# Attention in one-head loops, with 13 of 16 key tiles turned on VectorE and the exchange of their blocks shared out over DMA, GpSimd and ScalarE's queue

## The chip, the cores and the metric

One NeuronCore of a Trainium2 chip runs the whole kernel. The metric is the device time in microseconds (us). The kernel before took 3308.22 us, the median of three runs (3308.05 to 3309.66).

## The reference

`x` is (2, 2048, 256): two batches of 2048 tokens, 4096 tokens in all. The output is `x + attention(layernorm(x)) + moe(layernorm(x))`, all in float32.

    Q, K, V  = xn @ W_{Q,K,V} + b              # 16 heads of 64
    attn     = softmax(Q K^T / 8)              # per head, 2048 x 2048, no mask
    out      = sum over heads (attn V) W_O + b_O
    routed   = for each token, 8 of 32 experts, each row of `ye` times its weight, summed
    shared   = silu(xn Wg) * (xn Wu) Wd

The change concerns attention, and the summing of the 8 expert rows of each token, which GpSimd does beside it.

## The kernel before

The kernel has three stages: `project_and_route` (layer norm, Q, K, V, routing), `run_experts`, and `attend`. Q and K are kept in DRAM as a high and a low part, each float32r; the expert outputs are the rows of `ye`.

`attend` goes through 2 batches x 16 heads x 16 tiles of 128 queries: 512 slots, one per query tile. Each engine has its own program, and they meet at semaphores. `slots` (L846) says what a slot `s` of a head holds; work that lags is of earlier tiles. `over_heads` (L870) writes out the first and the last head of a batch and puts the 14 between into a loop of 7 rounds of two heads.

In one slot:

- TensorE (`body`, L1093): `transpose` turns the last 4 of the 16 key tiles of the probabilities of tile s-2 into bank 7 (L1056); `score` makes the 128 x 2048 scores with 8 matmuls of 512 columns (L1043), the early half into banks 0 and 1 or 4 and 5 by turns, the late half into banks 2 and 3; `project` multiplies the attention output of one tile of 13 slots ago with W_O, also in bank 7 (L1088), as two matmuls of 64 output partitions over 128 rows, which hold the sums over even and over odd key tiles; `times_v` (L1060) multiplies 4 key tiles with V for a group of 4 query tiles (512 queries), even key tiles into partitions 0 to 63 and odd ones into 64 to 127 of bank 6 (L1073).
- VectorE: the maximum over the early and the late half (L1164), the negated maximum (L1169), and the turning of 32 x 32 blocks of the first 12 key tiles of the tile before (`turn_blocks`, L1180). In one slot of four also two small operations on sums (L1195, L1198).
- ScalarE: scaling of the projected tile (L1136), the exponential of the late half (L1124), the copy of the transposed tiles out of bank 7 (`take`, L1112), the exponential of the early half, and in one slot of four the copy of the V product (L1152).
- GpSimd: adds the scaled tile to the accumulator `acc` (L1003), and `routed` (L967): in slots 0 to 7 of a head one indirect DMA each gathers rows of `ye` (L979), in slots 8 to 15 one such tile is multiplied by its weight (L987) and added (L989). Only in slots 8 and 12 does it wait for gathers.
- SyncE's queue: all loads, and `exchange` (L908). A VectorE block transpose stays within its 32 partitions, so block (r, c) of each tile has to go from partitions 32r to partitions 32c. For each group of 4 query tiles that is 16 DMAs of 32 partitions (L914), the 4 with r = c among them. The product with V waits for them one slot after its first part.

`wait_apart` (L37) is a wait followed by a separate semaphore instruction; L44 is its line.

Of the kernel before, what the change touches and what calls it, by code (L numbers as in the profile page):

```python
# [5 lines left out]
F32 = mybir.dt.float32  # L6
# [586 lines left out]
def run_experts(nc, io, scr, keep, ahead, start):  # L593
    with ExitStack() as stack:
# [28 lines left out]
        def _(sp):  # L623
# [9 lines left out]
            for part in range(2):  # L633
                load_k(sp, scr, start, 0, 0, 0, part)
# [126 lines left out]
MOVED = 12  # L761
# [3 lines left out]
LAST = OUT_LAG + TILES  # L765
PV_PLACES = ((12, 16), (0, 4), (4, 8), (8, 12))
# [3 lines left out]
PV_BANK, TURN_BANK = 6, 7  # L770
# [10 lines left out]
def load_k(sp, scr, start, b, h, side, part):  # L781

    keys = slice(part * T // 2, (part + 1) * T // 2)
    sp.dma_start(start["k_hl"][:, side, keys].bitcast(F32),
                 scr["k"][bass.ds(h * P, P), b * T + part * T // 2:b * T + (part + 1) * T // 2]
                 ).then_inc(start["k_loaded"][side], 16)


def attend(nc, io, scr, keep, ahead, start):
    with ExitStack() as stack:  # L790
# [8 lines left out]
        oT = ahead["xe"][:, 0, :, :].rearrange("p t d -> p (t d)").rearrange("p (g c) -> p g c", c=CH)  # L799
# [15 lines left out]
        scaled_sb = m.sb("scaled", [P, 2, D])  # L815
# [10 lines left out]
        exchanged = m.sems("exchanged", 2)  # L826
        turned = m.sem("turned")
# [18 lines left out]
        def slots(b, h):  # L846


            i, u = h if isinstance(h, tuple) else (0, h)
            h = 2 * i + u  # L850
            head = b * H + h
            pair, side = b * (H // 2) + i + u // 2, u % 2
            opens = b == 0 and isinstance(h, int) and h == 0
            for s in range(LAST if b == B - 1 and isinstance(h, int) and h == H - 1 else TILES):
# [4 lines left out]
                out = not opens or s >= OUT_LAG  # L859
                yield dict(  # L860
                    s=s, h=h, head=head, tile=tile, scores=s < TILES, side=side, pair=pair,
                    out_side=1 - side if s < OUT_LAG else side, out_pair=pair - 1 if s < OUT_LAG and not side else pair,
                    turn=(head * GROUPS + back[0], back[0] % 2, (s - 1) % GT) if turn and s <= TILES else None,
                    late=(not opens or s >= 2) and s <= TILES + 1,
                    pv=(head * GROUPS + back[1], back[1] % GROUPS, (s - PV_LAG) % GT)
                    if pv and s < PV_LAG + TILES else None,
                    out=(head * GROUPS + back[2], back[2] % GROUPS, (s - OUT_LAG) % GT, s < OUT_LAG)
                    if out and s < OUT_LAG + TILES else None)

        def over_heads(eng, body):  # L870
            for b in range(B):
                for s in slots(b, 0):
                    body(b, 0, s)
                with eng.Fori(0, H // 2 - 1) as i:
                    for u in (1, 2):
                        for s in slots(b, (i, u)):
                            body(b, (i, u), s)
                for s in slots(b, H - 1):
                    body(b, H - 1, s)

        def exchanges(head, g):

            return (head * (GROUPS // 2) + g // 2 + 1) * (QD * QD * 16)

        @block.sync
        def _(sp):
# [5 lines left out]
            def next_k(b, h, side, part):  # L892
                wait_apart(sp, late_scored, (b * H + h - 1) * TILES, sp_waits)
                load_k(sp, scr, start, b, h, side, part)
# [8 lines left out]
            def load_wo(b, h, side):  # L903
                wait_apart(sp, projected, (b * H + h - 1) * TILES + 1, sp_waits)
# [3 lines left out]
            def exchange(b, h, g):  # L908
# [9 lines left out]
            def store_out(b):  # L918

                for t in range(TILES):  # L920
                    sp.wait_ge(added, ((b + 1) * H - 1) * TILES + t + 1)
# [3 lines left out]
            def head_loads(b, h, side, before, following):  # L925

                next_q(b, h, 1)
                if before is not None:
                    exchange(*before, GROUPS - 1)
# [3 lines left out]
                load_wo(b, h, side)  # L933
# [3 lines left out]
                if following is not None:  # L937
                    next_k(*following, 1 - side, 0)
                exchange(b, h, 1)
                if following is not None:  # L940
                    next_q(*following, 0)
                    next_k(*following, 1 - side, 1)
                exchange(b, h, 2)

            for b in range(B):
                head_loads(b, 0, 0, (b - 1, H - 1) if b else None, (b, 1))
                with sp.Fori(0, H // 2 - 1) as i:
                    for u in (1, 2):
                        head_loads(b, 2 * i + u, u % 2, (b, 2 * i + u - 1), (b, 2 * i + u + 1))
                head_loads(b, H - 1, 1, (b, H - 2), (b + 1, 0) if b + 1 < B else None)  # L950
# [5 lines left out]
        def _(pool):  # L956
# [10 lines left out]
            def routed(b, s):  # L967

                k, h, n = s["s"] % K, s["h"], s["head"]
                part = k // (K // 2)  # L970
                if s["s"] < K:
                    if k == 0:
                        tile = b * TILES + h
                        nc.gpsimd.tensor_copy(g_index[:, :], keep["index"][:, bass.ds(tile, 1), :]
                                              .rearrange("p a k -> p (a k)"))
                        nc.gpsimd.tensor_copy(g_gain[:, :], keep["gain"][:, bass.ds(tile, 1), :]
                                              .rearrange("p a k -> p (a k)")).then_inc(g_staged, 1)
                        wait_apart(pool, g_staged, n + 1, pool_waits)
                    nc.gpsimd.indirect_dma_start(  # L979
# [303 lines left out]
```

## Time and profile before

| | us |
|---|---|
| median of 3 runs | 3308.22 |
| the profiled execution itself | 3313.78 |
| its span, first to last instruction | 3312.2 |
| TensorE busy (97% of the span) | 3196.9 |
| VectorE busy (77%) | 2544.1 |
| ScalarE busy (61%) | 2007.7 |
| GpSimd busy (44%) | 1454.5 |

Busy time is what an engine's own operations cover; waits, branches and the issue of DMAs on SyncE are not in it. The profiled execution took 5.6 us more than the median of the runs, 1.6 us of its time lie around the span.

### The profile page before, as it was taken

To read this page: it belongs to the slowest core of one execution; us is meant where nothing else is said; L and a number is where in the kernel's file an instruction comes from. 1 tells how busy PE (TensorE), PEld (TensorE's weight loads), DVE (VectorE), ACT (ScalarE), POOL (GpSimd) and SP (SyncE) were. 2 spreads that over 40 slices of the span, in tenths; PEclk is the share of its full clock that TensorE was granted. 3 is DMA by queue.
4 is the path that set the end of the run, shared out by engine and by line. 5 is a ranking of instruction groups with operands and counts; after the bars stand their busy time and mean duration, and the time that the engine had idled before them with its cause. 6 is when DMAs were issued, how large, how long until landed. Compare 5 with 4: busy or idle time off the path is not lost.

```text
span 3312.2 us, 54697 instructions
## 1 busy us (share of the span) xinstructions
PE 3196.9 (97%) x14467; PEld 1714.4 (52%) x14468; DVE 2544.1 (77%) x2917; ACT 2007.7 (61%) x3525; POOL 1454.5 (44%) x1795
## 2 busy tenths in 40 slices
PE   7799999998999999999999999999999999999998
PEld 3355444555555555555555555555555555555554
DVE  7612444234998989898988999898999899889995
ACT  4312320334676767676766777777777777777775
POOL 4677770013244444444444445544444444444443
PEclk9899999999999999999999999999999999999999
DMA  7613886665998989898988899999999999899997
GB/s 299 266 68 117 309 267 153 223 228 187 236 236 216 231 214 229 212 231 219 229 218 218 216 233 243 261 231 226 231 230 230 229 230 228 219 225 232 227 227 183
DMA packets 342733, 737.33 MB, mean 223 GB/s; under 512 B 129517, under 2 KB 177400, under 8 KB 342160
## 3 DMA queue, kind: packets, MB, share of 16 engines
q1 hardware_dynamic: 311056, 670.55, 76.9%
q0 software_dynamic: 31488, 64.51, 7.0%
q8 instruction: 88, 1.44, 0.2%
q14 instruction: 101, 0.83, 0.1%
HBM read 198.37 MB, written 159.51 MB: 108 GB/s over the span
## 4 chain that ended last, share of the span: by engine, by line
PE 70%; DVE 2%; issue 1%; SPq 1%; ACT 1%; DMA 0%; ACTq 0%; POOL 0%; DVEq 0%; POOLq 0%
PE at_ps L1043 27%; PE at_ps L1073 26%; PE at_ps L1056 9%; PE at_ps L1088 9%; DVE at_half_max L1164 1%; DVE at_blocks L1180 1%; SPq L914 1%; ACT at_prob L1124 0%; DMA at_v<-v_rows 0%; DMA at_moved<-at_blocks 0%; ACT at_scaled L1136 0%; DVE at_neg_max L1169 0%; ACT ahead_xe L1152 0%; SPq L905 0%; POOL at_acc L1003 0%
## 5 line engine op out<-in xcount | busy, mean ns | idle before, releaser
L1164 DVE TENSOR_REDUCE at_half_max<-at_ps 128x1 f32<-128x1024 f32 x1024 | 1206.6, 1219 | 250.9 <-PE at_ps L1043 249.0
L1124 ACT ACTIVATE at_prob<-at_ps,at_neg_max 128x1024 f32<-128x1024 f32 x1024 | 1145.3, 1118 | 333.7 <-DVE at_neg_max L1169 318.3
L1180 DVE STREAM_TRANSPOSE at_blocks<-at_prob 128x1536 f32<-128x1536 f32 x512 | 906.0, 1770 | 1.2 <-ACT at_prob L1124 1.2
L1043 PE MATMUL at_ps<-ahead_k_hl,ahead_q_hh 128*128 128x512 f32 x2048 | 854.4, 417 | 17.7 <-ACT at_prob L1124 10.8
L1003 POOL TENSOR_TENSOR at_acc<-at_acc,at_scaled 128x256 f32<-128x256 f32 x512 | 372.0, 727 | 1064.0 <-ACT at_scaled L1136 1064.0
L1043 PE MATMUL at_ps<-ahead_k_hl,ahead_q_ll 128*128 128x512 f32 x2048 | 810.2, 396 | 0.0
L1073 PE MATMUL at_ps<-at_moved,at_v 128*64 128x512 f32 x3072 | 726.8, 594 | 5.6 <-DMA at_moved<-at_blocks 4.3
L1136 ACT ACTIVATE at_scaled<-at_ps,at_inv 128x256 f32<-128x256 f32 x512 | 242.3, 473 | 354.1 <-PE at_ps L1088 340.0
L1056 PEld LDWEIGHTS at_ps<-keep_ident,at_prob 128*128 128x128 f32 x2048 | 216.1, 141 | 437.9 <-issue 425.5
L1043 PEld LDWEIGHTS at_ps<-ahead_k_hl,ahead_q_hh 128*128 128x128 f32 x2048 | 389.4, 190 | 88.2 <-ACT at_prob L1124 15.5
L1043 PEld LDWEIGHTS at_ps<-ahead_k_hl,ahead_q_ll 128*128 128x128 f32 x2048 | 390.4, 191 | 67.7
L1073 PEld LDWEIGHTS at_ps<-at_moved,at_v 128*64 128x64 f32 x3072 | 221.1, 137 | 282.4 <-issue 221.1
L1056 PE MATMUL at_ps<-keep_ident,at_prob 128*128 128x128 f32 x2048 | 337.0, 287 | 26.5 <-issue 21.1
L1088 PE MATMUL at_ps<-ahead_dn,ahead_xe 128*64 128x256 f32 x2048 | 336.1, 407 | 4.0 <-ACT at_scaled L1136 2.4
L1112 ACT COPY at_turned_sb<-at_ps 128x512 f32<-128x512 f32 x512 | 300.5, 587 | 44.4 <-PE at_ps L1056 35.2
L286 POOL DMA_INDIRECT xbuf<-pr_ebase,pr_stage_i x256 | 249.6, 975 | 100.3 <-issue 72.3
L1073 PE MATMUL at_ps<-at_turned_sb,at_v 128*64 128x512 f32 x1024 | 248.3, 604 | 2.5 <-issue 2.0
L1088 PEld LDWEIGHTS at_ps<-ahead_dn,ahead_xe 128*64 128x64 f32 x2048 | 102.9, 135 | 192.1 <-issue 187.9
L1124 ACT ACTIVATION_READ_ACCUMULATOR at_prob<-at_ps,at_neg_max 128x1 f32 x1024 | 201.6, 197 | 0.0
L979 POOL DMA_INDIRECT ahead_gu<-ye,at_g_index x128 | 133.8, 1045 | 115.0 <-POOL at_acc L1003 75.8
L979 POOL DMA_INDIRECT ahead_xe<-ye,at_g_index x128 | 131.6, 1028 | 108.8 <-POOL at_acc L1003 103.3
L645 POOL DMA_DIRECT2D ye<-ex_ye x32 | 24.2, 756 | 274.4 <-ACT ex_ye L664 271.2
(112 smaller groups left out, 2596.1 us busy)
## 6 DMA issues: line engine op xcount, KB each, us to landing
at_moved<-at_blocks SPq DMA_DIRECT2D x2048, 192.0 KB
ahead_k_hl<-k_parts SPq DMA_DIRECT2D x64, 512.0 KB, 8.0
ahead_q_hh<-q_parts SPq DMA_DIRECT2D x128, 256.0 KB, 5.6
ahead_q_ll<-q_parts SPq DMA_DIRECT2D x128, 256.0 KB, 6.4
xbuf<-pr_zeros SPq DMA_DIRECT2D x32, 512.0 KB, 5.1
q_parts<-pr_part_hi SPq DMA_DIRECT2D x64, 256.0 KB
q_parts<-pr_part_lo SPq DMA_DIRECT2D x64, 256.0 KB
k_parts<-pr_part_hi SPq DMA_DIRECT2D x64, 256.0 KB, 2.2
```

The costliest lines, as they stand in the source:

```text
L286: nc.gpsimd.indirect_dma_start(out=scr["xbuf"][:, :], out_offset=bass.IndirectOffsetOnAxis(ap=stage_i[:, q, k:k + 1], axis=0), in_=stage_x ...
L979: nc.gpsimd.indirect_dma_start(out=row(k), out_offset=None, in_=scr["ye"][:, :], in_offset=bass.IndirectOffsetOnAxis(ap=g_index[:, k:k + 1 ...
L1003: nc.gpsimd.tensor_tensor(acc[:, t, :], acc[:, t, :], scaled_sb[:, t % 2, :], ALU.add).then_inc(added, 1)
L1043: last = nc.tensor.matmul(ps[:, bank, :], q[:, g % 2, j * P:(j + 1) * P], k_hl[:, side, c * CH:(c + 1) * CH], start=first, stop=not first)
L1056: last = nc.tensor.transpose(ps[:, TURN_BANK, j * P:(j + 1) * P], prob[:, s["s"] % 2, t * P:(t + 1) * P], keep["ident"][:, :])
L1073: last = nc.tensor.matmul(ps[side:side + DH, PV_BANK, :], v[:, t, :], p_T, start=(place == 0 and t < tiles[0] + 2), stop=(place == GT - 1 ...
L1088: last = nc.tensor.matmul(ps[side:side + DH, TURN_BANK, 0:D], oT[:, g % 2, j * P + side:j * P + side + DH], wo[:, s["out_side"], :], start ...
L1112: nc.scalar.copy(turned_sb[:, parity, :, :, j, :], ps[:, TURN_BANK, 0:TURNED * P].rearrange("p (t r c) -> p t r c", r=QD, c=32)).then_inc( ...
L1124: nc.scalar.activation(prob[:, i % 2, half * 1024:(half + 1) * 1024], ps[:, banks[0]:banks[1], :].rearrange("p b c -> p (b c)"), ACT.Exp, ...
L1136: nc.scalar.activation(scaled_sb[:, t % 2, :], ps[:, TURN_BANK, 0:D], ACT.Identity, scale=inv[:, t:t + 1]).then_inc(scaled, 1)
L1164: nc.vector.tensor_reduce(half_max[:, i % 2, half:half + 1], ps[:, banks[0]:banks[1], :], AX.XY, ALU.max).then_inc(max_step, 1)
L1180: nc.vector.transpose(blocks[:, parity, :, j, :, :].rearrange("p c t k -> p t c k"), prob[:, (s["s"] - 1) % 2, 0:MOVED * P].rearrange("p ( ...
```

## The change

- The loop over the heads has one head per round, 14 rounds a batch. So both buffers of K (and of W_O) are loaded for each head: side 0 serves tiles 0 to 7, side 1 tiles 8 to 15.
- VectorE turns 13 of 16 key tiles, TensorE 3. TensorE turns them for two query tiles at once, in even slots, into banks 4 and 5, and ScalarE copies both in one instruction. Bank 7 is no longer used.
- The V product puts the first half of a group's queries into partitions 0 to 63 and the second half into 64 to 127: 256 columns per matmul and twice as many matmuls. The four slots take 3, 5, 4 and 4 key tiles.
- The projection of a query tile is one matmul over 64 rows with 128 output partitions. Two of them (rows 0 to 63 and rows 64 to 127) are made in each odd slot, into the two banks of the early half that is free.
- GpSimd copies the 4 diagonal blocks of a group, two in each even slot. It issues its gathers in pairs in even slots, and waits for each pair at the start of the next even slot.
- Of the 12 DMAs that are left, SyncE's queue issues the 6 with r = 0, 1 and ScalarE's queue the 6 with r = 2, 3, two at the end of each of three slots.

```diff
-MOVED = 12
+MOVED = 13
-PV_PLACES = ((12, 16), (0, 4), (4, 8), (8, 12))
+PV_PLACES = ((13, 16), (0, 5), (5, 9), (9, 13))
+GQ = GT // 2
+UPPER = ((2, 0), (3, 1), (2, 1), (3, 0), (2, 3), (3, 2))
-def load_k(sp, scr, start, b, h, side, part):
+def load_k(sp, scr, start, b, h, side):
...
-                with eng.Fori(0, H // 2 - 1) as i:
-                    for u in (1, 2):
-                        for s in slots(b, (i, u)):
-                            body(b, (i, u), s)
+                with eng.Fori(1, H - 1) as h:
+                    for s in slots(b, h):
+                        body(b, h, s)
...
-                for turn in range(QD):
+                for turn in range(1, QD):
                     for r, c in zip(ACROSS, ACROSS[turn:] + ACROSS[:turn]):
+                        if r >= QD // 2:
+                            continue
                         sp.dma_start(moved[c * 32:(c + 1) * 32, g % 2, r, :, :, :],
...
+            def diagonal(group, parity, r):
+
+                wait_apart(pool, blocks_done, GT * (group + 1), pool_waits)
+                wait_apart(pool, pv_done, GT * (group - 1), pool_waits)
+                for q in (r, r + 1):
+                    nc.gpsimd.tensor_copy(moved[q * 32:(q + 1) * 32, parity, q, :, :, :],
+                                          blocks[q * 32:(q + 1) * 32, parity, q, :, :, :]).then_inc(diag_done, 1)
+                    wait_apart(pool, diag_done, QD * group + q + 1, pool_waits)
...
+                if i % 2 == 0 and 0 < i <= K:
+                    part = (i - 1) // (K // 2)
+                    wait_apart(pool, gathered[part], s["head"] * 64 + 16 * (i - part * (K // 2)), pool_waits)
+                if s["diag"]:
+                    diagonal(*s["diag"])
...
+                    pe.wait_ge(diag_done, QD * (group + 1))
                     pe.wait_ge(exchanged[parity], exchanges(s["head"] - (1 if s["s"] < PV_LAG else 0), g))
...
+                    for half in range(2):
+                        side, queries = half * DH, slice(half * GQ, (half + 1) * GQ)
+                        p_T = (moved[:, parity, :, queries, t, :] if t < MOVED else
+                               turned_sb[:, parity, t - MOVED, :, queries, :])
+                        last = nc.tensor.matmul(ps[side:side + DH, PV_BANK, 0:GQ * P], v[:, t, :], p_T,
...
+                for n, g, j, half, behind in s["out"]:
...
+                    rows, queries = slice(half * DH, (half + 1) * DH), slice(j % GQ * P, (j % GQ + 1) * P)
+                    nc.tensor.matmul(out_of(s, half), oT[rows, g % 2, queries], wo[rows, g // 2, :],
+                                     start=True, stop=True).then_inc(projected, 1)
...
+            def send_upper(group, parity, part):
+
+                act.wait_ge(blocks_done, GT * (group + 1))
+                wait_pos(act, pv_done, GT * (group - 1))
+                for r, c in UPPER[2 * part:2 * part + 2]:
+                    nc.scalar.dma_start(moved[c * 32:(c + 1) * 32, parity, r, :, :, :],
+                                        blocks[r * 32:(r + 1) * 32, parity, c, :, :, :]).then_inc(exchanged[parity], 16)
```

GpSimd's order in an even slot is: the wait for the pair of gathers (slots 2, 4, 6, 8), two diagonal copies, then a pair of gathers (slots 0 to 6) or two times multiply and add (slots 8 to 14). In an odd slot it adds two scaled tiles. In the kernel before, the accumulator of scaled tiles `scaled_sb` has 2 buffers, in the changed one 4.

## Rows read from the trace of the kernel before

**Rows 1.** The page: busy time of each engine, then shares of the last chain.
```profile
PE 3196.9 (97%) x14467; PEld 1714.4 (52%) x14468; DVE 2544.1 (77%) x2917; ACT 2007.7 (61%) x3525; POOL 1454.5 (44%) x1795
...
PE 70%; DVE 2%; issue 1%; SPq 1%; ACT 1%; DMA 0%; ACTq 0%; POOL 0%; DVEq 0%; POOLq 0%
```
**Rows 2.** Windows: length, busy time of each engine, clock, DMA share over attention's slots.
```profile
805.00:3272.00 2467.00, 2427.01 (x12145) 1318.25 (x12143) 2202.88 (x2295) 1760.40 (x3177) 1086.43 (x1372) 0.99 0.92 227
```
**Rows 3.** Timeline of TensorE over a slot: start, length, instruction.
```profile
2273.06 0.66 PE L1056 MATMUL at_ps<-keep_ident,at_prob 128*128 128x128 f32 x4
...
2277.79 0.66 PE L1056 MATMUL at_ps<-keep_ident,at_prob 128*128 128x128 f32 x4
2278.20 0.47 PE L1043 MATMUL at_ps<-ahead_k_hl,ahead_q_hh 128*128 128x512 f32 x1
...
2279.90 0.39 PE L1043 MATMUL at_ps<-ahead_k_hl,ahead_q_ll 128*128 128x512 f32 x1
2280.22 0.65 PE L1088 MATMUL at_ps<-ahead_dn,ahead_xe 128*64 128x256 f32 x4
2280.71 1.94 PE L1073 MATMUL at_ps<-at_turned_sb,at_v 128*64 128x512 f32 x8
```
**Rows 4.** Timeline of VectorE in the first head, before V products begin.
```profile
833.29 2.31 DVE L1164 TENSOR_REDUCE at_half_max<-at_ps 128x1 f32<-128x1024 f32 x2
...
835.77 1.77 DVE L1180 STREAM_TRANSPOSE at_blocks<-at_prob 128x1536 f32<-128x1536 f32 x1
837.46 1.19 DVE L1164 TENSOR_REDUCE at_half_max<-at_ps 128x1 f32<-128x1024 f32 x1
```
**Rows 5.** Timeline: TensorE's first work after a loop's jump, batch 0, then batch 1.
```profile
1186.30 1.04 PE L1056 MATMUL at_ps<-keep_ident,at_prob 128*128 128x128 f32 x4 [3.64 <-issue]
...
2284.24 0.66 PE L1056 MATMUL at_ps<-keep_ident,at_prob 128*128 128x128 f32 x4 [1.60 <-ACT at_scaled L1136]
```
**Rows 6.** GpSimd's groups by form: its copies of 256 and of 8 elements.
```profile
L282 POOL COPY pr_ebase<-pr_xn 128x256 f32 x30 | 12.4, 412 | 0.0
...
L280 POOL COPY pr_stage_i<-keep_index 128x8 uint32 x30 | 6.4, 214 | 0.0
```
**Rows 7.** Timeline of GpSimd: a routed slot, a gather, two scatters in a row.
```profile
2340.43 0.73 POOL L1003 TENSOR_TENSOR at_acc<-at_acc,at_scaled 128x256 f32<-128x256 f32 x1 [1.94 <-ACT at_scaled L1136]
2341.46 0.93 POOL L987 TENSOR_SCALAR ahead_xe<-ahead_xe,at_g_gain 128x256 f32<-128x256 f32 x1 [0.30 <-POOL at_acc L1003]
2342.59 0.73 POOL L989 TENSOR_TENSOR at_acc<-at_acc,ahead_xe 128x256 f32 x1 [0.20 <-POOL ahead_xe L987]
...
2366.01 1.02 POOL L979 DMA_INDIRECT ahead_gu<-ye,at_g_index  x1 [0.88 <-POOL at_acc L1003]
...
389.39 0.97 POOL L286 DMA_INDIRECT xbuf<-pr_ebase,pr_stage_i  x1 [0.30 <-issue]
390.66 0.97 POOL L286 DMA_INDIRECT xbuf<-pr_ebase,pr_stage_i  x1 [0.30 <-issue]
```
**Rows 8.** DMA issues of one later head, then of the first: KB, us to landing.
```profile
DMA packets 5468, 17.16 MB, mean 226 GB/s; under 512 B 1376, under 2 KB 2016, under 8 KB 5467
...
at_moved<-at_blocks SPq DMA_DIRECT2D x64, 192.0 KB
...
ahead_k_hl<-k_parts SPq DMA_DIRECT2D x2, 512.0 KB, 7.6
...
ahead_xe<-ye,at_g_index POOLq DMA_INDIRECT x4, 6.4
...
ahead_xe<-ye,at_g_index POOLq DMA_INDIRECT x4, 3.3
```
**Rows 9.** Timeline of SyncE's queue: issues of the exchange in a row.
```profile
2283.89 8.09 SPq L914 DMA_DIRECT2D at_moved<-at_blocks  x12
```
**Rows 10.** The page's groups of ScalarE: scaling and copy of the transposed tiles.
```profile
L1136 ACT ACTIVATE at_scaled<-at_ps,at_inv 128x256 f32<-128x256 f32 x512 | 242.3, 473 | 354.1 <-PE at_ps L1088 340.0
...
L1112 ACT COPY at_turned_sb<-at_ps 128x512 f32<-128x512 f32 x512 | 300.5, 587 | 44.4 <-PE at_ps L1056 35.2
```

More of the change, by code:

```diff
@@ L630, in load @@
                     load_expert(sp, io, scr, ahead, e, q)
-            for part in range(2):
-                load_k(sp, scr, start, 0, 0, 0, part)
+            load_k(sp, scr, start, 0, 0, 0)
             load_q(sp, scr, start, 0, 0, 0)
@@ L995, in body @@
+                if i == 0 and not first and not last:
                     for q in range(4):
                         pool.wait_ge(base_loaded[q], 64 * (b + 1))
-                if s["out"]:
-                    group, g, j, behind = s["out"]
-                    n, t = group * GT + j, g * GT + j
-                    if h == 0 and not behind:
+                if b == 1 and first and i % GT == 1:
+                    g = i // GT
+                    for t in range(g * GT, (g + 1) * GT):
+                        pool.wait_ge(first_stored[t % 4], 16 * (t // 4 + 1))
+                        load_base(1, t)
@@ L1005, in body @@
                     wait_apart(pool, added, n + 1, pool_waits)
[L1006 removed]
+                    if b == 0 and last and not behind or b == 1 and first and behind:
                         store_first(t)
[L1008 to L1014 removed]
@@ L1076, in times_v @@
                 last.then_inc(pv_done, 1)
             def project(s):
-                group, g, j, behind = s["out"]
-                n = group * GT + j
-                if j == 0:
-                    pe.wait_ge(oT_done, group + 1)
-                    pe.wait_ge(wo_loaded[s["out_side"]], 16 * s["out_pair"] + 16)
-                wait_pos(pe, scaled, n)
-                if s["late"]:
-                    pe.wait_ge(copied, s["tile"] - 1)
-                for side in (0, DH):
-                    last = nc.tensor.matmul(ps[side:side + DH, TURN_BANK, 0:D],
-                                            oT[:, g % 2, j * P + side:j * P + side + DH], wo[:, s["out_side"], :],
-                                            start=True, stop=True)
@@ L1091, in project @@
-                last.then_inc(projected, 1)
+                for n, g, j, half, behind in s["out"]:
+                    if j == 0:
+                        pe.wait_ge(oT_done, s["pv_group"])
+                        pe.wait_ge(wo_loaded[g // 2], 16 * (s["head"] + (0 if behind else 1)))
+                    if half == 0:
+                        pe.wait_ge(early_exp, min(s["s"], TILES) + s["head"] * TILES)
+                        wait_pos(pe, scaled, n)
+                    rows, queries = slice(half * DH, (half + 1) * DH), slice(j % GQ * P, (j % GQ + 1) * P)
+                    nc.tensor.matmul(out_of(s, half), oT[rows, g % 2, queries], wo[rows, g // 2, :],
+                                     start=True, stop=True).then_inc(projected, 1)
@@ L1098, in body @@
                     score(s, 1)
-                if s["out"]:
-                    project(s)
+                project(s)
+                if s["taken"]:
+                    transpose(s)
                 if s["pv"]:
```

211 lines of the change are left out of this document (106 added, 105 removed).

## The prediction

> **What bounds the kernel now.** I read the page first: TensorE is busy for 97% of the span, and 70% of the chain that ended last is TensorE's own work [rows 1]. The windows then say the same of attention alone: 2427 of 2467 us, against 2203 for VectorE, 1760 for ScalarE, 1086 for GpSimd, with the DMA engines 92% busy [rows 2]. That window holds 511 slots, 4.83 us each. The timeline of a slot shows where TensorE's time lies: one slot begins at 2273.06 and the next at 2277.79, 4.73 us; in it the transposes take 0.41, the scores 2.02, the projection 0.49, and the V product the other 1.81 [rows 3]. The 0.10 us between 4.73 and 4.83 are mostly pauses at the loops' jumps. In batch 0 TensorE stood still for 3.64 us with nothing to wait for but its own instructions, and its first transposes then took 1.04 us in place of 0.66, as at 1.2 GHz; in batch 1 it waited 1.60 us on ScalarE [rows 5]. There are 6 such jumps in each batch. GpSimd, 44% busy, seems far from any limit. That is the reading I have to test, because it is the engine that the change loads most.
>
> **TensorE, four slots.** Scores 4 x 2.02 = 8.08, unchanged. Transposes: 12 instead of 16, at 0.41/4 = 0.10 each: 1.24. Projection: today 4 x 0.49, two matmuls of 256 columns side by side each time. The new pairs are side by side in rows and no longer in columns; the trace has no such pair. If they overlap likewise, two pairs cost 0.98, if they follow each other 2 x 0.9. I take 0.98, since they go to different rows and different banks as today's go to different columns. V product: the same columns in all, 4 x 1.81 = 7.24; the matmuls become half as long, and 256-column pairs already follow each other at 0.49 for two of them [rows 3], so the shorter form costs nothing that rows show. From the last score (2279.90) to the projection are 0.32 us, against 0.24 between scores: a change of shape costs 0.08. Odd slots get one more, 0.16 in four. Sum 8.08 + 1.24 + 0.98 + 7.24 + 0.16 = 17.7, or 4.43 per slot (4.65 if the pairs don't overlap).
>
> **VectorE.** In the first head, where it had no idle time, its slot was 833.29 to 837.46, 4.17 us [rows 4]. The transposes grow from 1536 to 1664 elements: 1.77/12 = 0.15 more. Two small operations in one slot of four add under 0.1 on average. So 4.4, beside TensorE's 4.43. As the two alternate and each waits for the other at times, I take 4.5 for both together.
>
> **ScalarE.** The copies of the transposed tiles become one of 768 elements for two slots, about 0.85 where two took 1.17, and the scalings stay [rows 10]. It issues 24 DMAs a head; SyncE's queue needs 8.09/12 = 0.67 us for each [rows 9]. Two follow the early exponential, in three slots of four. An issue keeps the sequencer busy and not the arithmetic, and the exponential that it follows lasts over a microsecond, so I cost it at nothing; uncovered it would be at most 6 x 0.67 = 4.0 us in four slots, of which the pause before the next maximum takes up about 1 us a slot. Still about 4.5 to 4.7. SyncE's queue gets shorter.
>
> **DMA.** A head moves 17.16 MB [rows 8]. 64 exchanges of 192 KB become 48 of 208 KB, 12.58 to 10.22 MB; the second load of K adds 1.05 and that of W_O 0.13: 16.0 MB. At 92% busy before, that is about 0.86 at the old pace and under 0.8 at 82 us a head. It bounds nothing. Each part of the exchange has more than a slot until it is read.
>
> **GpSimd.** Here the sum must be made in wall time, since each of its operations waits for the one before. Row by row:
> - Odd slot: two adds of 0.73 with 0.30 between them (two waits) and 0.15 ahead: 1.9 [rows 7].
> - Diagonal copies: 32 partitions, but 1664 elements in each. 256 elements took 0.412 and 8 took 0.214 [rows 6], that is 0.80 ns an element, so 0.412 + 1408 x 0.80 = 1.54. Short copies overlap a little, so the true slope is higher. I take 1.6. The ends: 1.4, were all of the 0.214 overlap, and 6.0, were it as slow per element as the multiply (0.93 for 256 [rows 7]); the copy's own row is the nearest. Two copies, 0.2 between, and 0.45 for the waits ahead of them (0.30 is seen for two): 3.85 per even slot.
> - Even slot 8 to 14: two multiplies and adds, 2 x (0.2 + 0.93 + 0.2 + 0.73) = 4.1.
> - Even slot 0 to 6: 0.88 until the first gather, 1.28 until the second (the scatters' spacing), 1.02 for it [rows 7]: 3.2.
>
> So two slots cost 3.85 + 4.1 + 1.9 = 9.85 in the second half of a head and 3.85 + 3.2 + 1.9 = 8.95 in the first, with 0.4 for the index copies: 75.6 us for 16 slots. TensorE needs 16 x 4.5 = 72. GpSimd is then the bound, although its busy share would look like 75%. The diagonal copies of a group must be done before the second of the four V products; a lag that grows each half head soon reaches that wait.
>
> To this comes a new wait. Before, gathers were waited for only half a head later, so their landing cost nothing. Now the pair issued in slots 0, 2, 4, 6 is waited for at the start of the next even slot, ahead of the copies. The second gather starts 3.85 + 0.88 + 1.28 = 6.0 us into its pair of slots; the next pair begins when it has landed, at 6.1 + L. Landing took 6.4 us in a later head and 3.3 in the first, when the DMA engines were less loaded [rows 8]. The new load lies between, and the second gather queues behind the first: I take L = 4.5, with 3.3 and 6.4 as ends. Four pairs cost 4 x 10.6 = 42.4. Queued behind this wait are the copies, the adds and with them the V product.
>
> **Sum.** A head costs GpSimd 42.4 + 4 x 9.85 + 0.4 = 82.2 us, 5.14 a slot; 511 slots 2625, less 8 for the first head, where most of this is missing: 2617 against 2467 [rows 2], +150. The pauses at the jumps are in the 2467 and need no term of their own; with TensorE waiting for GpSimd they gain nothing. The stages before attention stay. 3313.8 + 150 = 3464 for the profiled execution, whose time was 5.6 us over the median of the runs; so 3458.
>
> **Rivals.**
> - Landing is quick (L under 3). Then no gather is waited for, a head costs 75.6, and 511 slots 2414 - 8: -61, **3247**. For it: fewer and more evenly spread exchanges. Against it: even the first head had 3.3. The Trainium skill, "DMA: Bandwidth & Descriptors", section "Anatomy of one DMA", gives a DMA of GpSimd's queue about 2.0 us plus its bytes over 436 GB/s, an estimate of 2.3 us for 128 KB, and thus this rival's time. The rows of this trace stand above that figure throughout.
> - TensorE and VectorE remain the bound at 4.5: 511 x 4.5 = 2300, -167, **3141**. That needs a copy on GpSimd of at most (1.6 - 10.2/16) = 1.0 us at L = 4.5. For it: with only 32 of 128 partitions a copy may be cheaper than its elements say. Against it: the rows know only 128 partitions, and elements per partition should count. With row pairs that do not overlap this becomes 4.7, about 3240.
> - Landing as slow as in the later heads (L = 6.4) with copies of 1.7: 4 x 12.7 + 4 x 10.05 + 0.4 = 91.4 a head, +440, **3750**. Three queues instead of two compete with the gathers.
> - The point between faster and slower is a GpSimd head of about 77.5 us (2467/511 x 16 and the first head's 8 us spread): L = 3.3 with copies of 1.6, or L = 4.5 with copies of 1.3.
>
> **How the numbers follow.** The forecast with GpSimd and its gathers as the bound has 0.52, its own range 3330 to 3600 (L 3.5 to 5.5, copies 1.5 to 1.7). Quick landing 0.14, TensorE as the bound 0.22 (with the unpaired projection), slower landing 0.08, a balance near zero 0.04. A measurement of this kernel tells about 0.2% from no change. Faster 0.36, same 0.04, slower 0.60. Both signs hold much, so the range that leaves out 2 in 10 reaches from TensorE's case to 3600.
>
> **What would show it.** Right: copies on GpSimd of 1.5 to 1.7 us; GpSimd's idle time put down to the landing of gathers, in slots 2 to 8; V products waiting for GpSimd's copies, once per group; TensorE's slots at 4.4 between those waits; the even halves of a head (slots 0 to 7) slower than slots 8 to 15; TensorE at 85 to 90% busy. Wrong: copies under 1.1 us, or GpSimd waiting for the scaled tiles as it does now, or V products waiting for the exchange's DMAs or ScalarE.

## The result and the profile after

The changed kernel takes 3685.36 us (median of 4 runs, 3668.17 to 3694.97), the kernel before beside it 3308.14 us: ratio 1.1135, 95% interval 1.1093 to 1.1176. The direction was forecast, the size was not: 3685 lies above the range, which ended at 3600. The profiled execution has a span of 3683.6 us.

The page of the changed kernel, busy times and the chain that ended last:

```profile
PE 3237.7 (88%) x17028; PEld 1972.3 (54%) x17028; DVE 2652.1 (72%) x2917; ACT 1867.8 (51%) x3269; POOL 2259.2 (61%) x2307
...
POOL 27%; DMA 21%; PE 17%; issue 10%; POOLq 2%; ACT 0%; DVE 0%; ACTq 0%; DVEq 0%
POOL at_moved L1009 16%; DMA ahead_xe<-ye,at_g_index 10%; PE at_ps L1103 9%; DMA ahead_gu<-ye,at_g_index 8%; PE at_ps L1071 7%; DMA at_moved<-at_blocks 3%; POOL at_acc L1034 3%; POOL at_acc L1001 3%; POOL ahead_gu L998 2%; POOL ahead_xe L99
```

TensorE had 70% of this chain before [rows 1], now GpSimd and the DMAs that it waits for lead. Attention's slots as one window (same columns as [rows 2]):

```profile
805.00:3640.00 2835.00, 2465.10 (x14615) 1568.30 (x14615) 2302.26 (x2287) 1615.58 (x2912) 1873.81 (x1871) 0.93 0.74 183
```

The window grew from 2467 to 2835 us, +368 of the +377 in all. The DMA engines fell from 92% to 74%, and the mean granted clock from 0.99 to 0.93. A slot took 5.57 us on average, 89.1 us a head (from the starts of VectorE's late maxima, 511 intervals; all slot times below are made so). Over the heads, slots 1, 5 and 9 took 9.27, 7.02 and 11.59 us, and most of the others 4.54 to 4.7: the time was lost in a few long stops. What GpSimd and TensorE waited for (engine, line and cause; us in total, times, longest):

```profile
POOL at_moved L1009 <- DMA ahead_xe<-ye,at_g_index: 230.8, 58, 8.6
POOL at_moved L1009 <- DMA ahead_gu<-ye,at_g_index: 202.6, 59, 5.2
```
```profile
PE at_ps L1103 <- POOL at_moved L1009: 243.0, 68, 11.9
PE at_ps L1103 <- DMA at_moved<-at_blocks: 93.4, 28, 4.4
```

GpSimd stood 433 us before its diagonal copies until gathers had landed, 13.5 us a head. TensorE's V products stood 243 us for those copies, about twice a head. They stood another 93 us for DMAs of the exchange, 28 times and always in slot 1, a sign that the prediction had listed under "wrong". GpSimd's timeline over one head's gathers shows the loop of the stall:

```profile
2310.25 1.57 POOL L1009 COPY at_moved<-at_blocks 32x1664 f32<-32x1664 f32 x1 [0.54 <-POOL at_acc L1034]
2311.99 1.57 POOL L1009 COPY at_moved<-at_blocks 32x1664 f32<-32x1664 f32 x1 [0.17 <-POOL at_moved L1009]
...
2315.20 1.16 POOL L993 DMA_INDIRECT ahead_gu<-ye,at_g_index  x1 [0.91 <-POOL at_g_gain L987]
2316.66 1.03 POOL L993 DMA_INDIRECT ahead_gu<-ye,at_g_index  x1 [0.30 <-issue]
2317.71 0.75 POOL L1034 TENSOR_TENSOR at_acc<-at_acc,at_scaled 128x256 f32<-128x256 f32 x1
2318.79 0.73 POOL L1034 TENSOR_TENSOR at_acc<-at_acc,at_scaled 128x256 f32<-128x256 f32 x1 [0.34 <-POOL at_acc L1034]
2323.70 1.56 POOL L1009 COPY at_moved<-at_blocks 32x1664 f32<-32x1664 f32 x1 [4.18 <-DMA ahead_gu<-ye,at_g_index]
...
2334.88 1.57 POOL L1009 COPY at_moved<-at_blocks 32x1664 f32<-32x1664 f32 x1 [2.76 <-DMA ahead_gu<-ye,at_g_index]
...
2346.82 1.56 POOL L1009 COPY at_moved<-at_blocks 32x1664 f32<-32x1664 f32 x1 [3.50 <-DMA ahead_xe<-ye,at_g_index]
```

Each pair of slots is paced by the landing: 13.45, 11.18 and 11.94 us from copy to copy, and 13.52 for the fourth. The DMA view of the whole run gives the landing (count, median us):

```profile
ahead_gu<-ye,at_g_index POOLq DMA_INDIRECT x128, 5.8
ahead_xe<-ye,at_g_index POOLq DMA_INDIRECT x128, 5.7
```

These medians are over both gathers of a pair, but GpSimd waits for the second one. From issue to landing the second took 6.2 us in the mean of all 128 pairs, and GpSimd's copies began 0.4 us after it had landed.

### The profile page after: what moved, and what is told of

The parts are those of the page before. It is cut to its first block, busy times and chain, and to the rows that moved or that the text cites. A ratio compares the mean times of both kernels' runs of the same rounds, so it can differ in the third digit from the quotient of the medians.

```text
span 3683.6 us, 61395 instructions
## 1 busy us (share of the span) xinstructions
PE 3237.7 (88%) x17028; PEld 1972.3 (54%) x17028; DVE 2652.1 (72%) x2917; ACT 1867.8 (51%) x3269; POOL 2259.2 (61%) x2307
## 4 chain that ended last, share of the span: by engine, by line
POOL 27%; DMA 21%; PE 17%; issue 10%; POOLq 2%; ACT 0%; DVE 0%; ACTq 0%; DVEq 0%
POOL at_moved L1009 16%; DMA ahead_xe<-ye,at_g_index 10%; PE at_ps L1103 9%; DMA ahead_gu<-ye,at_g_index 8%; PE at_ps L1071 7%; DMA at_moved<-at_blocks 3%; POOL at_acc L1034 3%; POOL at_acc L1001 3%; POOL ahead_gu L998 2%; POOL ahead_xe L998 2%; PE at_ps L1083 1%; PE at_ps L1118 1%; POOLq L44 1%; POOL ahead_xe L993 1%; POOLq L43 1%
## 5 line engine op out<-in xcount | busy, mean ns | idle before, releaser
L1103 PE MATMUL at_ps<-at_moved,at_v 128*64 128x256 f32 x6656 | 912.7, 424 | 349.6 <-POOL at_moved L1009 243.0
L1009 POOL COPY at_moved<-at_blocks 32x1664 f32<-32x1664 f32 x512 | 802.1, 1567 | 557.4 <-DMA ahead_xe<-ye,at_g_index 230.8
L1218 DVE STREAM_TRANSPOSE at_blocks<-at_prob 128x1664 f32<-128x1664 f32 x512 | 974.3, 1903 | 200.9 <-POOL at_moved L1009 148.9
L1071 PE MATMUL at_ps<-ahead_k_hl,ahead_q_hh 128*128 128x512 f32 x2048 | 882.7, 431 | 19.2 <-ACT at_prob L1152 8.7
L1103 PEld LDWEIGHTS at_ps<-at_moved,at_v 128*64 128x64 f32 x6656 | 497.1, 150 | 689.5 <-issue 308.9
L1139 ACT COPY at_turned_sb<-at_ps 128x768 f32<-128x768 f32 x256 | 204.8, 800 | 740.5 <-PE at_ps L1083 740.5
L1083 PE MATMUL at_ps<-keep_ident,at_prob 128*128 128x128 f32 x1536 | 211.3, 274 | 1.8 <-ACT at_prob L1152 1.8
L1083 PEld LDWEIGHTS at_ps<-keep_ident,at_prob 128*128 128x128 f32 x1536 | 182.5, 141 | 41.0 <-issue 9.8
L1103 PE MATMUL at_ps<-at_turned_sb,at_v 128*64 128x256 f32 x1536 | 194.8, 389 | 0.5 <-issue 0.5
L1118 PE MATMUL at_ps<-ahead_dn,ahead_xe 64*128 64x256 f32 x1024 | 179.9, 424 | 14.8 <-ACT at_scaled L1164 1.0
```

What stands on the lines that cost most here:

```text
L1009: nc.gpsimd.tensor_copy(moved[q * 32:(q + 1) * 32, parity, q, :, :, :], blocks[q * 32:(q + 1) * 32, parity, q, :, :, :]).then_inc(diag_don ...
L1071: last = nc.tensor.matmul(ps[:, bank, :], q[:, g % 2, j * P:(j + 1) * P], k_hl[:, side, c * CH:(c + 1) * CH], start=first, stop=not first)
L1083: last = nc.tensor.transpose(ps[:, EARLY[1][0] + a, j * P:(j + 1) * P], prob[:, a, t * P:(t + 1) * P], keep["ident"][:, :])
L1103: last = nc.tensor.matmul(ps[side:side + DH, PV_BANK, 0:GQ * P], v[:, t, :], p_T, start=(place == 0 and t == tiles[0]), stop=(place == GT ...
L1118: nc.tensor.matmul(out_of(s, half), oT[rows, g % 2, queries], wo[rows, g // 2, :], start=True, stop=True).then_inc(projected, 1)
L1218: nc.vector.transpose(blocks[:, parity, :, j, :, :].rearrange("p c t k -> p t c k"), prob[:, (s["s"] - 1) % 2, 0:MOVED * P].rearrange("p ( ...
```

## The experiments

The runs were made on several chips. On two of them (the first seven experiments) the kernel before itself took 3445 and 3492 us; there attention only began at 935 to 987 us instead of 800, so the extra time lies ahead of the part studied. The mean slot of attention is therefore the better number to compare across runs, the ratio within one. Three comparisons below still cross chips: e1 with e10, e6 with e8, and e5 with e9. Those of the changed kernel with e13, of e9 with e14 and of e11 with e12 were made where the kernel before took 3308 to 3311 us. The mean slot of e2 is that of its longest execution (3581 us; the other three took 3525 to 3576).

| run | chip's kernel before, us | ratio, 95% interval | mean slot, us |
|---|---|---|---|
| changed kernel | 3308 | 1.1135 [1.1093, 1.1176] | 5.57 |
| e1_gathers_apart | 3445 | 1.0639 [1.0616, 1.0663] | 5.25 |
| e2_diag_dma | 3445 | 1.0318 [1.0244, 1.0392] | 5.10 |
| e3_both | 3445 | 1.0265 [1.0227, 1.0304] | 5.04 |
| e4_two_heads | 3492 | 1.0518 [1.0480, 1.0555] | 5.16 |
| e5_twelve | 3492 | 1.0203 [1.0158, 1.0248] | 4.96 |
| e6_no_gathers | 3492 | 1.0220 [1.0203, 1.0237] | 4.99 |
| e7_half_copies | 3492 | 1.0214 [1.0186, 1.0243] | 4.98 |
| e8_sooner | 3311 | 0.9783 [0.9767, 0.9799] | 4.69 |
| e9_queue | 3311 | 1.0043 [1.0027, 1.0060] | 4.87 |
| e10_apart | 3311 | 1.0295 [1.0277, 1.0312] | 5.03 |
| e11_both_ways | 3311 | 1.0078 [1.0062, 1.0095] | 4.88 |
| e12_one_head | 3308 | 0.9807 [0.9793, 0.9820] | 4.69 |
| e13_sooner_alone | 3308 | 1.0793 [1.0764, 1.0822] | 5.36 |
| e14_twelve_one_head | 3308 | 0.9792 [0.9779, 0.9805] | 4.70 |

### Taking the landing, and the copies, away

**e1_gathers_apart**: the four copies of a group together in slots 0, 4, 8, 12, the gathers four at a time behind them in slots 0 and 4, waited for four slots later.

```diff
-                if i % 2 == 0 and 0 < i <= K:
-                    part = (i - 1) // (K // 2)
-                    wait_apart(pool, gathered[part], s["head"] * 64 + 16 * (i - part * (K // 2)), pool_waits)
+                if i % GT == 0 and 0 < i <= K:
+                    wait_apart(pool, gathered[i // GT - 1], s["head"] * 64 + 64, pool_waits)
```

> The changed kernel with the landing of the gathers taken off GpSimd's path and nothing else: the four diagonal copies of a group stand together in every fourth slot, the gathers go out four at a time right behind them (slots 0 and 4) and are waited for four slots later. Theory A (the changed kernel is bound by GpSimd's own work, 75.6 us a head, plus the landing waits, some 13.5 us a head): the landing waits vanish, a head falls from 89 to about 75 to 77 us, the whole to 3240 to 3300 us, and TensorE still waits for the copies once per group. Theory B (the landing waits only stand where something else, such as the exchange's DMAs or the half clock of TensorE, is the bound): the time stays above 3550.

**e2_diag_dma** sends the diagonal blocks by SyncE's DMAs as before and keeps the waits for pairs of gathers; **e3_both** also moves these waits to slots 8 and 12.

```diff
-                for turn in range(1, QD):
+                for turn in range(QD):
...
-                        if r >= QD // 2:
+                        if turn and r >= QD // 2:
```

> The changed kernel with the 4 diagonal blocks sent by SyncE's queue like the others, no copies on GpSimd; the waits for the pairs of gathers stay. Theory A: GpSimd has about 8.5 us of work and landing in two slots of the first half head and 6.4 in the second, both under TensorE's 9, so TensorE and VectorE bound it at 4.5 us a slot: 3130 to 3180 us. Theory B (DMA or the new waits on TensorE bind): over 3400, with V products waiting for the exchange, which now has a third more blocks.

> Diagonal blocks by DMA as in e2 and the gathers waited for only where they are used (slots 8 and 12), as in the kernel before. Theory A: the same as e2 within 0.5%, as neither wait is on the path any more: 3130 to 3180 us, faster than the kernel before by about 5%. If landing still held up the adds of the scaled tiles in e2, e3 is faster than e2 by more than 0.5%.

In e1 the waits for landing went, and the slot fell from 5.57 to 5.25, but not to GpSimd's own 75.6 us a head (4.73): it came to 84, with slots 1 and 5 at 8.42 and 6.69. In e2 and e3 GpSimd makes no copies, and in e3 no landing is waited for until the rows are used either, yet slot 1 still took 9.47 and 9.16, and V products waited 148 us in e3 for DMAs of the exchange. TensorE at 4.5 was not reached, and something in slot 1 was left that is neither copies nor landing. As e3's DMA engines showed 99% busy at 245 GB/s, I took the bytes for it:

```profile
1000.00:3500.00 2500.00, 2343.64 (x14360) 1502.19 (x14358) 2192.39 (x2225) 1575.30 (x2845) 1054.79 (x1332) 0.97 0.99 245
```

### Bytes, or something else?

**e4_two_heads** is e3 with two heads a round, so K and W_O are loaded once a head; **e5_twelve** is e4 with

```diff
-MOVED = 13
+MOVED = 12
...
-PV_PLACES = ((13, 16), (0, 5), (5, 9), (9, 13))
+PV_PLACES = ((12, 16), (0, 4), (4, 8), (8, 12))
```

> The kernel of e3_both (13 tiles, diagonals by DMA, gathers waited for late) with the loop over two heads again, so K and W_O are loaded once a head: 19.34 - 1.05 - 0.13 = 18.16 MB a head. Theory that the bytes bind once GpSimd is relieved: at the 245 GB/s that e3_both reached a head takes 74 to 76 us, a slot 4.65 to 4.75 us, DMA engines still 98 to 99% busy, ratio to the kernel before about 0.98. Rival, that the load of K just ahead of the exchange delays it by its place in the queue: slots of 4.55, DMA share under 0.96, ratio 0.96. Rival, that the DMA issues on ScalarE or TensorE itself set 5.0: no change from e3_both, ratio 1.03.

> e4_two_heads with 12 tiles turned on VectorE and 4 on TensorE, as in the kernel before: 17.16 MB a head, as before. Theory of the bytes: 17.16 MB at 245 GB/s are 70 us, so TensorE becomes the bound, with one more transpose of 0.10 a slot: 4.6 to 4.7 a slot, ratio 0.965 to 0.975, DMA share 0.95 to 0.97, and faster than e4_two_heads or equal. Rival, that fewer tiles on TensorE pay whatever the DMA does: e4_two_heads is faster than this one by 0.1 us a slot (1.5%).

Both forecasts of the theory of the bytes were missed, 4.65 to 4.75 for e4 and 4.6 to 4.7 for e5. Though 1.2 MB a head lighter, e4 was even slower than e3 (5.16 against 5.04). That alone does not refute the bytes, since the longer loop also brings back the pause at its jump: slot 15 took 6.01 in e4 and 4.55 in e3. What speaks against them is that the stop had moved: slot 13 took 8.44 and slot 1 4.87 in e4. In e5 slots 13 and 15 took 6.51 and 6.31; it was faster than e4, so the rival expected of it fell as well. e14 below settles the point.

**e6_no_gathers** and **e7_half_copies** change only GpSimd's part of the changed kernel. After the first head e6 leaves out the gathers and the waits for them, so the rows added are not those of the tokens; e7 leaves out half of each diagonal copy, so half of these blocks keep old values.

```diff
+                    if s["s"] < K and not opening:
+                        continue
...
+                if b == 0 and first and i % 2 == 0 and 0 < i <= K:
```
```diff
-                    nc.gpsimd.tensor_copy(moved[q * 32:(q + 1) * 32, parity, q, :, :, :],
+                    nc.gpsimd.tensor_copy(moved[q * 32:(q + 1) * 32, parity, q, 0:tiles, :, :],
```

> The changed kernel without its gathers after the first head, and without the waits for them (left out: the routed rows that are added are not those of the tokens). Theory that the landing of the gathers is the error of the forecast: GpSimd's two slots cost 3.85 + 1.9 + 0.3 = 6.05 in the first half of a head and 9.85 in the second, 64 us a head, so TensorE sets the time at 4.55 to 4.7 a slot, ratio to the kernel before 0.95 to 0.975. Rival, that landing only covers something else (ScalarE's DMA issues, the exchange): slots stay above 5.0, ratio above 1.03.

> The changed kernel with half of each diagonal block copied after the first head of a batch (left out: the diagonal blocks of two of a group's four query tiles keep old values). Theory, GpSimd in wall time: each copy loses 832 elements x 0.80 ns = 0.67 us, 16 a head, 89.1 - 10.7 = 78.4 us a head, 4.9 a slot, ratio about 1.02, and the waits for landing stay 12 to 14 us a head. Rival, that a 32-partition copy has a price that doesn't go by its elements: copies stay near 1.5 us and the time near that of the changed kernel, 1.10. Rival, that the landing waits grow as the copies shrink: ratio above 1.06.

Both lost the stops in slots 5 and 9, and both ended at the same place, 4.99 and 4.98: slot 1 took 9.43 and 9.68, all others 4.54 to 5.24. So the stops in slots 5 and 9 go when either the landing or half of the copying is taken away, and slot 1 has another cause. e7's ratio is the one expected, but not for the reason given: its landing waits were 215 us, 6.7 a head instead of 12 to 14, and TensorE's slot 1 made up the rest. The halved copies took 0.87 us each, where the whole one took 1567 ns: 0.84 ns an element. The mean of 886 ns in this line also holds the first head's whole copies:

```profile
L1009 POOL COPY at_moved<-at_blocks 32x832 f32<-32x832 f32 (+1 forms) x512 | 453.4, 886 | 359.1 <-DMA ahead_gu<-ye,at_g_index 113.5 <-DMA ahead_xe<-ye,at_g_index 101.7 <-DVE at_blocks L1218 50.6
```

The timeline of e7 around slot 1 of a head names the cause:

```profile
2083.21 1.83 ACTq L1172 DMA_DIRECT2D at_moved<-at_blocks  x2
...
2089.64 1.16 ACTq L1172 DMA_DIRECT2D at_moved<-at_blocks  x2
...
2094.47 0.34 SPq L784 DMA_DIRECT2D ahead_k_hl<-k_parts  x1
...
2095.55 0.61 ACTq L1172 DMA_DIRECT2D at_moved<-at_blocks  x1
...
2104.95 4.54 PE L1103 MATMUL at_ps<-at_moved,at_v 128*64 128x256 f32 x20 [2.88 <-DMA at_moved<-at_blocks]
```

SyncE's six blocks of the group had left by 2085. ScalarE's six leave by twos in three slots; the last leaves at 2095.55, 1.1 us behind the load of 1 MB of K, and lands 9.4 us later, 2.88 us after TensorE wants it. Then TensorE's product takes 4.54 us, where the same 20 matmuls took 2.38 at 2083.39 of the same head: 634 ns a matmul instead of 379. The granted clock of 2105 to 2109 was 0.50, so 1.2 instead of 2.4 GHz. A wait of 2.9 us thus cost 5.

That the load of K counts, and not the late place alone, shows within e6, e7 and the changed kernel. ScalarE's last two DMAs leave at the same place in slots 3, 7, 11 and 15, but a load of K goes out just ahead of them only in slot 15, and TensorE waited for the exchange in slot 1 alone, 28 times for 90 to 93 us in each of the three. In e4 and e5, with two heads a round, the load just ahead stands in slot 11, and most of these waits lie in slot 13: 82 us in e4 (44 in slot 5 and 32 in slot 9), 42 us in e5.

### Sending sooner

In **e8_sooner** (on e6), **e10_apart** (on e1) and **e13_sooner_alone** (on the changed kernel itself) ScalarE sends three DMAs in each of two slots:

```diff
-                    if (not opens or s >= 5) and s < TILES + 5 and (s - 5) % GT < 3 else None,
+                    if (not opens or s >= 5) and s < TILES + 5 and (s - 5) % GT < 2 else None,
...
-                for r, c in UPPER[2 * part:2 * part + 2]:
+                for r, c in UPPER[3 * part:3 * part + 3]:
```

> e6_no_gathers (the changed kernel without its gathers, the same part left out), and ScalarE's queue sends its six DMAs of a group three each in two slots instead of two each in three. In e6_no_gathers and e7_half_copies nearly all time over 4.7 a slot lies in slot 1, 9.4 to 9.7 us, where TensorE waits about 3 us for an exchange and then runs at half clock: the last two DMAs of group 2 leave ScalarE's queue in slot 15, right behind the second load of K (1 MB), and land 9 us later. Theory that the third of ScalarE's sendings comes too late for its reader: slot 1 falls to 4.6 to 5.5, the mean slot from 4.99 to 4.70 to 4.75, ratio to the kernel before about 0.98. Rival, that the load of K holds up whatever is in flight then: slot 1 stays above 8. Rival, that three issues in a row delay ScalarE's next exponential: all slots of two in four grow by 0.5 or more.

> e1_gathers_apart (all gathers, waited for four slots later, all four copies on GpSimd), and ScalarE's sendings in two slots instead of three. Theory of two separate costs: slot 1 loses its wait of the exchange as in e8_sooner, 3 to 4 us a head, so 5.25 becomes 5.0 to 5.05; what is left over 4.75 (GpSimd's own sum of 75.6 us a head) is GpSimd waiting where four copies and four gathers in a row make it late. Ratio 1.02 to 1.03. Rival, that GpSimd alone sets e1's time: no change, 1.06.

> The changed kernel, and only ScalarE's sendings three each in two slots. Its price over the kernel before was 11.3%. Theory that the late third sending costs it something of its own beside the landing of the gathers (e1_gathers_apart to e10_apart gained 3.4 points, on different chips): 1.08 to 1.10, and slot 1 falls from 9.3 us by 2 to 4. Rival, that GpSimd's head of 89 us sets the time whatever the exchange does, so that ScalarE's delay lies beside it: 1.105 to 1.115, slot 1's time only moves to slots 5 and 9.

In e8 slot 1 fell from 9.43 to 5.27 and the mean to 4.69: the theory held, with its number, though e8 and e6 ran on different chips. In e13, the one change in the changed kernel itself and on a chip like the first, slot 1 fell from 9.27 to 5.97 and the ratio from 1.1135 to 1.0793, just under the range expected; slot 5 rose from 7.02 to 9.48, since part of GpSimd's lateness comes out there. What is left is GpSimd's sum:

```profile
POOL at_moved L1009 <- DMA ahead_xe<-ye,at_g_index: 196.4, 61, 7.5
POOL at_moved L1009 <- DMA ahead_gu<-ye,at_g_index: 132.4, 54, 4.8
```

329 us in 32 heads are 10.3 a head; with 75.6 that is 85.9, measured 85.8. In the changed kernel it is 13.5 + 75.6 = 89.1, measured 89.1. So the landing waits themselves shrank by 3.2 us a head when ScalarE sent sooner, and that is the whole gain of e13. The gathers landed sooner: the second of a pair took 5.4 us in the mean instead of 6.2, and four pairs times 0.8 are 3.2. This was not for a lighter load, since in e13 the DMA engines were 77% busy at 190 GB/s, in the changed kernel 74% at 183. That the late sendings and the gathers are then less often in the DMA engines together is my reading; no run separates it. e10 takes these waits out too: 1.0295, 80.5 us a head, where four copies in a row make V products wait 170 us for GpSimd.

### One queue, and the jump of the loop

**e9_queue** is e5 with all 16 DMAs of a group on SyncE's queue. **e11_both_ways** is e10 with two heads a round, and with two of the four diagonal blocks copied by GpSimd and two sent by DMA. **e12_one_head** is e11, and **e14_twelve_one_head** is e9, each with one head a round again.

```diff
+                        if (r >= QD // 2) == (turn > 0):
+                            continue
...
-                for q in range(QD):
+                for q in range(QD // 2):
```

> e5_twelve (12 tiles, two heads a round, all 16 blocks by DMA, 17.16 MB a head) with all of the exchange on SyncE's queue as in the kernel before; against that kernel only the query halves, the projection by row pairs and the transposes by two are left. Theory that ScalarE's late sendings cost e5_twelve its waits in slots 13 and 15: they go, slots 4.55 and 4.81 by turns, mean 4.70 to 4.75, ratio 0.97 to 0.985. Rival, that the DMA engines are the bound: 17.16 MB at the pace of this chip take as long as in the kernel before, ratio 0.995 to 1.005 and waits for at_moved spread over the slots.

> A version meant to beat both: 13 tiles, two heads a round, gathers in fours waited for four slots later, two diagonal blocks of a group copied by GpSimd and two by DMA, ScalarE's sendings in two slots. GpSimd's sum is 75.6 - 8 x 1.9 = 60 us a head, the bytes 16.0 - 1.18 + 8 x 0.21 = 16.5 MB. If the costs add up as the theory says, neither binds, slots of 4.6 to 4.7, ratio 0.955 to 0.975. Rival, that the DMA engines bind near 17 MB whoever issues: 0.99 to 1.01.

> e11_both_ways with one head a round as in the changed kernel: 16.5 + 1.18 = 17.7 MB a head. In e11_both_ways every second head loses 5 to 6 us in its slot 15, with half clock behind it, where TensorE waits for nothing but its instructions at the loop's jump. Theory that this pause goes with the shorter loop: mean slot 4.88 - 0.17 = 4.71 or a little less, ratio 0.975 to 0.985, faster than both kernels. Rival, that the larger bytes (DMA share above 0.95) bring waits for the exchange back: slots 1 and 13 over 6 us, ratio 0.99 to 1.02.

> e9_queue (12 tiles, all 16 blocks by DMA on SyncE's queue, gathers waited for late) with one head a round: 17.16 + 1.18 = 18.3 MB a head. Theory of the jump: slot 15 falls from 6.87 to 4.6, mean slot 4.70 to 4.75, ratio 0.975 to 0.985. Rival of the bytes: 18.3 MB at 240 GB/s take 76 us a head, 4.77 a slot, so the gain is lost to the DMA engines, ratio 0.985 to 1.00.

From e5 to e9 slot 13 went from 6.51 to 4.70, which fits ScalarE's late sendings as the cause there too (the chip changed as well). Yet e9 is 0.4% slower than the kernel before, as the rival of the bytes had it; but not for the bytes. The same holds for e11, meant to beat both kernels at 0.955 to 0.975 and measured at 1.0078. Its heads take 75.5 and 80.8 us by turns, and the difference lies in slot 15 of every second one, at the loop's jump:

```profile
2430.68 1.95 PE L1104 MATMUL at_ps<-at_moved,at_v 128*64 128x256 f32 x16
2437.13 0.79 PE L1073 MATMUL at_ps<-ahead_k_hl,ahead_q_hh 128*128 128x512 f32 x1 [4.50 <-issue]
2437.72 0.63 PE L1073 MATMUL at_ps<-ahead_k_hl,ahead_q_ll 128*128 128x512 f32 x1
...
2440.27 0.63 PE L1073 MATMUL at_ps<-ahead_k_hl,ahead_q_ll 128*128 128x512 f32 x1
```

TensorE stands 4.50 us with nothing to wait for, 12 times in the run, and then works at half clock (granted 0.50 from 2437 to 2442; 0.63 a matmul, else 0.39). That slot 15 took 10.56 us instead of 4.55. The page counts the DMAs that fetch TensorE's instructions, queue 8 (packets, MB, share), first in e9, then in e14:

```profile
q8 instruction: 159, 2.61, 0.4%
```
```profile
q8 instruction: 31, 0.51, 0.1%
```

With one head a round the fetching and the pause are gone: slot 15 takes 4.56, the mean falls from 4.87 to 4.70, the ratio from 1.0043 to 0.9792 (e11 to e12: 1.0078 to 0.9807). The kernel before has such pauses too, shorter ones [rows 5]: 88 packets, slot 15 at 5.66 us in the mean, where e9 has 6.87. The query halves double the number of V matmuls in the body, which is the likely reason for the longer ones, though no run takes the halves alone. And e14 moves 18.3 MB a head and waits for the exchange 9.2 us in all:

```profile
805.00:3199.00 2394.00, 2377.26 (x15166) 1575.02 (x15166) 2198.83 (x2292) 1647.83 (x2918) 1083.09 (x1368) 1.00 0.97 248
```
```profile
PE at_ps L1097 <- DMA at_moved<-at_blocks: 9.2, 4, 4.6
```

97% busy and 248 GB/s, and TensorE still has 2377 of 2394 us. So the DMA share of 99% in e3 did not by itself prove a bound; what counts is when a block leaves.

Both e12 and e14 came out as their theories had it and are faster than both kernels, by 2% over the kernel before (3242.36 and 3238.38 against 3307.79). They keep the change's one-head loop, query halves, row-pair projection and transposes by two. e14 needs neither GpSimd's copies nor ScalarE's queue.

## Why the prediction was wrong

**Right.** The reading of GpSimd as the new bound in wall time, at 61% busy. Its copies took 1.57 us (I took 1.6), a routed pair of slots 10.0 (9.85), and the head without landing 75.6, in the changed kernel as in e13. V products waited for GpSimd's copies, about twice a head where I had four times. On GpSimd the first half of a head was the slower one, as I had it, 49.3 against 40.4 us; by TensorE's slots the halves came out alike, 44.6 and 44.5 us, since the lag that the gathers leave comes out in slot 9. TensorE's row pairs overlap: the four matmuls of an odd slot take 0.63 us until the V product starts (e9's and e14's timelines; I had 0.49, and 0.9 if they followed each other).

**The step that failed** is "I take L = 4.5, with 3.3 and 6.4 as ends". The four pairs of the head shown took 50.1 us, where I had 42.4: (50.1 / 4) - 6.1 gives L = 6.4, my upper end, and the second gathers of these pairs took 5.3 to 7.7 us to land, 6.4 in the mean. Over all heads they took 6.2, so the sum lacks 4 x (6.2 - 4.5) = 6.8 us a head. What is missing is 89.1 - 82.2 = 6.9 us a head, 32 heads 221 us: nearly the whole of 3685 - 3458 = 227. I had argued that a lighter DMA load brings the landing between the two rows of before [rows 8]. The load did become lighter (74% instead of 92%), but the landing hardly shorter: a median of 5.7 us for the gathers into `ahead_xe`, 6.6 before. And the busy share does not order it: in e14, at 97%, the medians were 5.6 and 5.7, in e13, at 77%, about 4.8. Why a gather takes what it takes stays open beyond what e13 shows. The Trainium skill, "DMA: Bandwidth & Descriptors", section "Anatomy of one DMA", would give 2.3 us for these 128 KB, an estimate; the trace does not agree, with medians of 5.7 and 5.8.

**The second failed step** is "so I cost it at nothing" of ScalarE's six DMAs, with "Each part of the exchange has more than a slot until it is read". I had priced the issues and not the moment of the last one: in slot 15 of a head, behind the second load of K, it had 6.5 us until TensorE wanted it and took 9.4 (e7). In the changed kernel this is worth 3.4 of the 11.3 points (e13), that is 113 of the 377 us, and about half of what my sum lacked. It is not a cost beside L, but part of the error in L: all of it goes through the landing waits, 13.5 to 10.3 us a head. The stop in slot 1 lies beside GpSimd's chain there and shows as a cost of its own only where GpSimd is relieved (e6 to e8). The Trainium skill, same page, section "Issuing engines are not separate DMA queues", says that issuing on several engines only saves the sequencer's time. e5 and e9 agree, and the sharing itself came to cost 0.09 a slot (4.96 against 4.87, on different chips), since ScalarE's program can only send at set places.

**The rivals.** The one that came is "Landing as slow as in the later heads", with a chance of 0.08: its L = 6.4 with copies of 1.6 instead of its 1.7 gives a head of 89.8 us and about 3701, measured 3685. Its reason, that three queues compete with the gathers, no run takes alone; e13 shows that the moment of ScalarE's sendings matters, with all three in use. "Quick landing" and "TensorE and VectorE as the bound" had 0.36 together. The second is not to be had at 3141 even with both causes gone: e12's undisturbed heads take 74.1 us, 4.63 a slot, where I had 4.5, because a slot with 13 tiles takes 4.55 to 4.80. Its direction was right, but its condition, a cheaper copy on GpSimd, is not enough: e7 with copies of 0.87 us was 2% slower than the kernel before. Only with ScalarE's sendings made sooner as well is the kernel faster (e8, e12).

**A gain I had set aside**: "the pauses at the jumps ... need no term of their own". In the changed kernel they are gone (30 packets of instructions for TensorE instead of 88), but GpSimd's stops hid the gain, so for this kernel the step held; between e9 and e14 the shorter loop is worth 2.5%.

## What to carry to other kernels

- A wait placed ahead of an in-order engine's other work costs the landing time of the last transfer waited for, each time. Take the slowest row of the trace for it, not the middle, unless a row shows that the load is what sets it.
- When DMAs move to the queue of a computing engine, write down for each when it can leave and when it is read. Its last one counts, and what large load goes out just ahead of it.
- Judge parts of a change apart. Here GpSimd's share and ScalarE's share of the exchange lost over 13% and hid other parts that together gain 2%.

## What the runs showed of the hardware

- A pause of 3 to 4.5 us on TensorE costs more than its length, 1.3 to 1.8 times as much here: after 2.88 us of waiting, 20 matmuls took 4.54 us instead of 2.38 (e7), 5.0 us lost in all; after 4.50 us of nothing the scores took 0.63 each instead of 0.39 (e9), 6.0 us lost in all. The granted clock was 0.50 behind both. After 1.66 us of idle time in the same head of e7 the matmuls kept their 379 ns.
- A loop body with more TensorE instructions went with a dearer jump: 4.50 us and 159 packets in the run with two heads of 256-column products a round (e9), no pause and 31 packets with one (e14), 88 packets and shorter pauses with two heads of 512-column products (the kernel before).
- The DMA engines carried 248 GB/s at 97% busy through all of attention with four waits (e14), and a gather of 128 KB landed there in 5.6 to 5.7 us, no later than at 74% busy and 183 GB/s in the changed kernel (5.7 to 5.8). The busy share says little about the time that one transfer takes.
- A copy on GpSimd over 32 partitions goes by its elements per partition: 0.87 us for 832, 1.57 for 1664.
